# The last normalisation's mean and variance, on ScalarE in two passes and one step later

## The reference, cut to what matters

```python
x = _layernorm(x + decoder_layer(x))        # inside: h = ln(x + attn); ln(h + ffn(h))
x = _layernorm(x + expert_layer(x))         # the change concerns this norm
def _layernorm(x, axis=-1, eps=1e-05):
    m = jnp.mean(x, axis=axis, keepdims=True)
    v = jnp.var(x, axis=axis, keepdims=True)
    return (x - m) / jnp.sqrt(v + eps)
```

## Time and profile before

| | |
|---|---|
| median of 3 runs | 413.44 us (413.07 to 413.97) |
| the profiled execution's own time | 413.25 us |
| its span, first to last instruction | 411.5 us |
| PE / DVE / POOL / ACT busy | 91% / 80% / 61% / 52% |

### The profile page before, as it was taken

The page is one execution under the profiler, slowest core; times in us unless marked ns, Lnnn a source line. Parts: engine busy times, 40 slices in busy tenths (PEclk is TensorE's granted clock), DMA queues, the critical chain, the costliest instruction groups (busy, mean ns, idle before and its releaser), DMA issues. The chain is left out here.

```text
span 411.5 us, 6629 instructions
## 1 busy us (share of the span) xinstructions
PE 374.3 (91%) x2082; PEld 261.3 (64%) x2082; DVE 330.2 (80%) x789; ACT 215.9 (52%) x397; POOL 252.3 (61%) x431
## 2 busy tenths in 40 slices
PE   8897889788999999989998999899998998999992
PEld 3554556475847776677757884787567764955651
DVE  3649965699589987999799978998899979844543
ACT  2240316327844487527951896358652883276450
POOL 2017235896189836984599538983798459955231
PEclk9999999899999999999999999999999999999998
DMA  8236006500090006400370018100730045000000
GB/s 262 115 70 161 1 2 142 140 2 0 18 220 21 0 2 156 126 2 0 87 195 2 1 37 209 40 0 2 171 86 0 2 105 125 2 2 26 0 27 26
DMA packets 19875, 26.59 MB, mean 65 GB/s; under 512 B 1664, under 2 KB 9984, under 8 KB 19840
## 3 DMA queue, kind: packets, MB, share of 16 engines
q1 hardware_dynamic: 19696, 25.96, 24.7%
q10 hardware_dynamic: 144, 0.21, 0.2%
HBM read 7.29 MB, written 2.10 MB: 23 GB/s over the span
## 5 line engine op out<-in xcount | busy, mean ns | idle before, releaser
L892 POOL TENSOR_TENSOR prod<-cum_kv,q_fac 128x512 f32<-128x512 f32 x64 | 92.3, 1453 | 31.5 <-DVE cum_kv L1098 24.7
L412 PEld LDWEIGHTS pO<-s_wor,prod 128*128 128x128 f32 x512 | 62.9, 193 | 33.1 <-POOL prod L892 20.5
L412 PE MATMUL pO<-s_wor,prod 128*128 128x128 f32 x512 | 70.2, 283 | 13.3 <-POOL prod L892 13.2
L1092 DVE TENSOR_TENSOR kv<-k,vb 128x512 f32<-128x512 f32 x64 | 52.9, 827 | 6.7 <-DMA vb<-vs 6.7
L879 POOL TENSOR_TENSOR var_eps<-mv,s_con 128x4 f32<-128x4 f32 x32 | 9.5, 297 | 64.5 <-DVE mv L1120 64.5
L1098 DVE TENSOR_TENSOR_SCAN cum_kv<-p_ones,cum_kv,kv 128x512 f32<-128x512 f32 x32 | 40.5, 1275 | 0.6
L1098 DVE TENSOR_TENSOR_SCAN cum_kv<-p_ones,kv 128x512 f32<-128x512 f32 x32 | 38.6, 1214 | 0.5
L687 ACT ACTIVATE v<-pA,s_att 128x512 f32<-128x512 f32 x7 | 4.8, 687 | 62.4 <-PE pA L348 62.4
L517 PE MATMUL pY<-s_moe,gel 128*128 128x128 f32 x256 | 33.0, 276 | 0.0
L517 PEld LDWEIGHTS pY<-s_moe,gel 128*128 128x128 f32 x256 | 31.0, 192 | 2.9 <-issue 1.9
L882 POOL TENSOR_TENSOR rstd<-var_eps,s_con 128x4 f32<-128x4 f32 x32 | 32.5, 1016 | 0.0
(11 more groups left out here) (165 smaller groups left out, 813.1 us busy)
## 6 DMA issues: line engine op xcount, KB each, us to landing
vb<-vs SPq DMA_DIRECT2D x64, 256.0 KB, 4.7
xT<-x_t SPq DMA_DIRECT2D x8, 256.0 KB, 4.3
xt<-x SPq DMA_DIRECT2D x8, 256.0 KB, 5.0
out<-y SPq DMA_DIRECT2D x7, 256.0 KB, 2.3
s_moe<-moe_w SPq DMA_DIRECT2D x1, 836.0 KB, 10.1
s_wor<-wo_rep SPq DMA_DIRECT2D x1, 512.0 KB, 8.2
s_ffn<-ffn_w SPq DMA_DIRECT2D x1, 512.0 KB, 8.7
s_con<-consts SPq DMA_DIRECT2D x1, 502.0 KB, 4.8
```

Source lines behind the costliest of these rows:

```text
L412: mm = pe.matmul(pO3[:, s, :], prod[:, m % 4, s * P:(s + 1) * P], s_wor[:, m, :], start=False, stop=(m == DH - 1), skip_group_check=True)
L892: pool.tensor_tensor(prod[:, m % 4, :], cum_kv[t.par][:, m, :], q_fac[t.par][:, :], ALU.mult).then_inc(prod_ready, 1)
L1092: dve.tensor_tensor(kv[:, m % 3, :], k[t.par][:, :], vb[:, m, :], ALU.mult).then_inc(kv_ready, 1)
```

## The change

Tiles 0 to 4 get their norm 3 in another way and one step later (e = s-3). DVE still writes the residual, now into one of two buffers by the tile's parity, but takes no moments of it. In the next step ACT copies the four pieces into the output buffer y (which is overwritten later) with the sum over the features as accumulated output, POOL makes -mean and a bias from the sums, ACT squares the centred pieces with an accumulated output, which is the variance, POOL makes the inverse standard deviation and the shift, and ACT normalises. Tiles 5, 6 and 7 keep the old way.

```diff
+LATE_NORMS = TILES - 3
...
-        res = [None, None] + [sb(f"res{i}", [P, SUB, P]) for i in (2, 3)]
+        res = [None, None, sb("res2", [P, SUB, P]), None]
+        res3 = [sb(f"res3_{i}", [P, SUB, P]) for i in range(2)]
...
+        def late_norm(t):
+            return t.n < LATE_NORMS
+        def vector_norms(t, i):
+            return t.n - LATE_NORMS if i == 3 else t.n
... SP, step
-                if D: store(d)
+                if E and late_norm(e): store(e)
+                if D and not late_norm(d): store(d)
... ACT
+            def sum_residual(t):
+                act.wait_ge(res_ready[3], t.n + 1)
+                act.wait_ge(y_free[t.par], 16 * (t.slot_uses + 1))
+                for s in range(SUB):
+                    act.activation(y[t.par][:, s, :], res3[t.par][:, s, :], ACT.Copy,
+                                   accum_out=r_sum[:, s:s + 1]).then_inc(rsum_ready, 1)
+            def square_residual(t):
+                act.wait_ge(rsum_ready, SUB * (t.n + 1))
+                act.wait_ge(rbias_ready, t.n + 1)
+                for s in range(SUB):
+                    act.activation(y[t.par][:, s, :], res3[t.par][:, s, :], ACT.Square, bias=r_bias[:, s:s + 1],
+                                   scale=P ** -0.5, accum_out=r_var[:, s:s + 1]).then_inc(rvar_ready, 1)
... ACT, last_step
-                relu(d, 2); relu(d, 3)
-                normalise(c, 2); x2T_out(c); gate_exp(c)
+                relu(d, 2)
+                sum_residual(e)
+                relu(d, 3)
+                normalise(c, 2); x2T_out(c)
+                square_residual(e)
+                gate_exp(c)
...
                 u1T_out(c); gated_constant(c); udT_out(c)
+                normalise(e, 3)
... ACT, step
                 if A: q_out(a)
+                if E: sum_residual(e)
                 if D: relu(d, 3)
                 if A: k_out(a)
                 if C: normalise(c, 2); x2T_out(c)
+                if E: square_residual(e)
                 if A: v_out(a)
...
-                if D: normalise(d, 3)
+                if E: normalise(e, 3)
+                if D and not late_norm(d): normalise(d, 3)
... POOL
+            def residual_mean(t):
+                pool.wait_ge(rsum_ready, SUB * (t.n + 1))
+                wait(pool, norm_ready[3], SUB * t.n)
+                pool.tensor_tensor(neg_mean[3][:, :], r_sum[:, :], con("mean"), ALU.mult).then_inc(negmean_ready[3], 1)
+                pool.tensor_tensor(r_bias[:, :], r_sum[:, :], con("root"), ALU.mult).then_inc(rbias_ready, 1)
+            def residual_inverse_std(t):
+                pool.wait_ge(rvar_ready, SUB * (t.n + 1))
...                 (var+eps, pow and shift as in inverse_std)
... POOL, step
-                if B: product(b, 3); product(b, 4); product(b, 5); product(b, 6); product(b, 7); shifted_x(b)
+                if B: product(b, 3); product(b, 4)
+                if E and late_norm(e): residual_mean(e)
+                if B: product(b, 5); product(b, 6); product(b, 7); shifted_x(b)
                 if D: constant_residual(d)
                 if B: inverse_std(b, 0); scaled_h(b); h_residual(b)
+                if E and late_norm(e): residual_inverse_std(e)
                 if A: e_normal(a); attention_input(a)
-                if D: inverse_std(d, 3)
+                if D and not late_norm(d): inverse_std(d, 3)
                 if B: inverse_std(b, 1)
... DVE, expert_residual
-                wait(dve, norm_ready[3], SUB * t.n)
+                wait(dve, norm_ready[3], SUB * (t.n - 1))
... DVE, step
-                if D: piece_moments(d, 3)
+                if D and not late_norm(d): piece_moments(d, 3)
                 if A: values(a)
-                if D: join_moments(d, 3)
+                if D and not late_norm(d): join_moments(d, 3)
```

More of the change, by code:

```diff
@@ L31 @@
            "prefer": (896, 928), "mhalf": (928, 932), "lneps": (932, 936), "restart": (936, 1000),
-           "minus": (1000, 1004)}
+           "minus": (1000, 1004), "mean": (1004, 1008), "root": (1008, 1012)}
 ROWS = {"bo": 0, "g1": 1, "b1n": 2, "b2": 3, "g2": 4, "b2n": 5, "bffn": 6}
@@ L79, in build @@
         s_att = sb("s_att", [P, 415])
-        s_con = sb("s_con", [P, 1004])
+        s_con = sb("s_con", [P, 1012])
         s_wor = sb("s_wor", [P, DH, P])
@@ L154, in build @@
         x_b2n = sb("x_b2n", [P, SUB, P])
-        res = [None, None] + [sb(f"res{i}", [P, SUB, P]) for i in (2, 3)]
+        res = [None, None, sb("res2", [P, SUB, P]), None]
+        res3 = [sb(f"res3_{i}", [P, SUB, P]) for i in range(2)]
+        r_sum, r_bias, r_var = (sb(n, [P, SUB]) for n in ("r_sum", "r_bias", "r_var"))
         stats = [sb(f"stats{i}", [P, SUB, 6]) for i in range(4)]
@@ L192, in build, with residual @@
         res[0], res[1] = pO3, pY3
+        def residual(t, i):
+            return res3[t.par] if i == 3 else res[i]
+        def late_norm(t):
+            return t.n < LATE_NORMS
+        def vector_norms(t, i):
+            return t.n - LATE_NORMS if i == 3 else t.n
         def v_bank(t):
@@ L249, in build @@
         shift_ready = [sem(f"shift_ready{i}") for i in range(4)]
+        rsum_ready, rbias_ready, rvar_ready = sem("rsum_ready"), sem("rbias_ready"), sem("rvar_ready")
         norm_ready = [sem(f"norm_ready{i}") for i in range(4)]
@@ L316, in step @@
             def step(s):
-                a, b, c, d = s.plus(1), s, s.plus(-1), s.plus(-2)
-                A, B, C, D = a.exists(), b.exists(), c.exists(), d.exists()
+                a, b, c, d, e = s.plus(1), s, s.plus(-1), s.plus(-2), s.plus(-3)
+                A, B, C, D, E = a.exists(), b.exists(), c.exists(), d.exists(), e.exists()
                 if B: spread_vs(b, 4); spread_vs(b, 5); spread_vs(b, 6)
@@ L729, in normalise @@
                 for s in range(SUB // 2 if (i == 3 and t.n == TILES - 1) else SUB):
-                    act.activation(dst[:, s, :], res[i][:, s, :], ACT.Identity, bias=shift[i][:, s:s + 1],
+                    act.activation(dst[:, s, :], residual(t, i)[:, s, :], ACT.Identity, bias=shift[i][:, s:s + 1],
                                    scale=rstd[i][:, s:s + 1]).then_inc(norm_ready[i], 1)
+            def sum_residual(t):
[10 more added lines that the diff above has]
+                                   scale=P ** -0.5, accum_out=r_var[:, s:s + 1]).then_inc(rvar_ready, 1)
             def h_out(t):
@@ L830, in last_step @@
             def last_step(b):
-                c, d = b.plus(-1), b.plus(-2)
-                relu(d, 2); relu(d, 3)
-                normalise(c, 2); x2T_out(c); gate_exp(c)
+                c, d, e = b.plus(-1), b.plus(-2), b.plus(-3)
+                relu(d, 2)
[4 more added lines that the diff above has]
+                gate_exp(c)
                 normalise(b, 0); h_out(b); gelu(b, 0); gelu(b, 1)
@@ L875, in _ @@
         def _(pool):
+            def residual_mean(t):
[5 more added lines that the diff above has]
+                pool.wait_ge(rvar_ready, SUB * (t.n + 1))
+                pool.tensor_tensor(var_eps[3][:, :], r_var[:, :], con("lneps"), ALU.add).then_inc(vareps_ready[3], 1)
+                pool.wait_ge(vareps_ready[3], t.n + 1)
+                pool.tensor_tensor(rstd[3][:, :], var_eps[3][:, :], con("mhalf"), ALU.pow).then_inc(rstd_ready[3], 1)
+                pool.wait_ge(negmean_ready[3], t.n + 1)
+                pool.wait_ge(rstd_ready[3], t.n + 1)
+                pool.tensor_tensor(shift[3][:, :], neg_mean[3][:, :], rstd[3][:, :], ALU.mult).then_inc(shift_ready[3], 1)
             def inverse_std(t, i):
-                pool.wait_ge(mv_ready[i], SUB * (t.n + 1))
+                pool.wait_ge(mv_ready[i], SUB * (vector_norms(t, i) + 1))
                 wait(pool, norm_ready[i], SUB * t.n)
@@ L1109, in piece_moments @@
                         dve.wait_ge(res_ready[2], SUB * t.n + s + 1)
-                    dve.bn_stats(stats[i][:, s, :], res[i][:, s, :]).then_inc(stats_ready[i], 1)
+                    dve.bn_stats(stats[i][:, s, :], residual(t, i)[:, s, :]).then_inc(stats_ready[i], 1)
             def moments(t, i):
@@ L1116, in join_moments @@
             def join_moments(t, i):
-                dve.wait_ge(stats_ready[i], SUB * (t.n + 1))
+                dve.wait_ge(stats_ready[i], SUB * (vector_norms(t, i) + 1))
                 dve.memset(fence[:, :], 0.0)
@@ L1203, in expert_residual @@
                 dve.wait_ge(x2c_ready, t.n + 1)
-                wait(dve, norm_ready[3], SUB * t.n)
+                wait(dve, norm_ready[3], SUB * (t.n - 1))
                 for s in range(SUB):
-                    ins = dve.scalar_tensor_tensor(res[3][:, s, :], pY3[:, s, :], gate_sum[t.par][:, s:s + 1],
+                    ins = dve.scalar_tensor_tensor(res3[t.par][:, s, :], pY3[:, s, :], gate_sum[t.par][:, s:s + 1],
                                                    x2c[:, s, :], ALU.mult, ALU.add)
@@ L1236, in closing @@
                 for s in range(SUB // 2, SUB):
```

(4 more changed lines are left out.)

## The result

The changed kernel takes 418.07 us (median of 4, 417.22 to 418.58) against 413.3 us (413.07 to 413.97): ratio 1.0111, interval 1.009 to 1.0132. The forecast was 416.3 us, with a range of 414.9 to 417.9. A second series gave 417.29 us (median of 5, 416.81 to 418.25) beside 413.37 us: 1.0096, 1.008 to 1.0112. The profiled execution took 417.96 us, 4.7 us more than that of the kernel before, with a span of 416.2 us.

What follows compares the result with a forecast made beforehand. The prediction took DVE's scans and PE to limit each step in turn. 413.25 us + 0 for the steps + 2.87 for the last step gave 416.1, by the median 416.3 us; range 414.9 to 417.9.

Steps and rivals of the forecast that it cites:

- What bounds: In a middle step: DVE's scans limit at about 256 to 268 us, PE from 268 to 295 us.
- What comes off DVE: Norm 3's moments: 1.43 us per late tile, 7.2 us over five; counted as 0 because both following waits end with PE.
- rival B: DVE's relief counts because scans begin earlier; in full -7.2 us, 409.1 us; chance 0.04 in full or enough to win.
- Sums: Four accumulating copies on ACT before relu(d, 3), steps 3 to 6: 0.5 us each, 2.0 us together, cost 0.
- the cover: PE's 1.12 us of waiting for POOL's products hides ACT's four sums up to 2.5 us per step.
- Squares: Four accumulating squares on ACT after x2T_out: 2.0 us, hidden while v_out waits for PE; cost 0.
- Buffers and constants: Second residual buffer removes a wait never open; eight more constant columns add under 0.1 us to one load: 0.
- The new wait: Last step: POOL's inverse_std(5, 3) waits for ACT's tile 4, delaying tile 7's norm 1; 2.87 us, bounds 2.0 and 3.4.
- The pauses: PE's new waits ahead of x2_T in the last step: 1.2, 0.8 and 1.3 us, with work between.
- D: Rival, chance 0.05: PE's new pauses in the last step lower the clock; about 1.7 us more, 418.0 us.
- A: Rival, chance 0.08: ACT's four sums cost more than 2.5 us; at 0.8 us a piece, 419.1 us in all.
- C: Rival, chance 0.05: tile 7 does not feel the last step's wait since PE holds it back anyway; 413.4 us.

Runs made afterwards that it cites:

- e4: The changed kernel with norm 3's bn_stats and bn_aggr back on DVE for tiles 0 to 4, into buffers nobody reads: 416.95 us.
- e6: The changed kernel with ACT's four summing activations issued three times, the additional sets into spare buffers: 417.70 us.
- e8: The changed kernel with no late tile, keeping the two residual buffers, weaker wait and extra constant columns: 413.42 us, ratio 0.9996.
- e1: The changed kernel with ACT's normalise(4, 3) in the last step moved ahead of u1T_out(6): 413.38 us, ratio 0.9989; repeated, 413.42 us.
- e2: The changed kernel with POOL's inverse_std(b, 1) placed ahead of inverse_std(d, 3): 415.34 us, ratio 1.0038.
- e7: The changed kernel with four late tiles instead of five: 416.66 us, ratio 1.0078.
- e5: The changed kernel with ACT's four summing activations issued twice, the additional set into spare buffers: 417.68 us.

## Why the forecast was right in kind and 1.8 us short

- What bounds: PE behind DVE's two waits. Right (e4). What comes off DVE was put too high, 1.43 us a tile for a measured 1.1: I had added up busy times of instructions that overlap. Step 1 of the kernel before, which has no norm 3, already had waits of 1.82 and 1.10 us. Since the term counted as 0, it cost nothing; the bound of -7.2 us in rival B would have been -5.4.
- Sums: 0.29 us a piece, not 0.5. The read of the accumulator, which I bounded by the 202 ns of table_probe, is there with 190 ns but overlaps its neighbours. Cost in the step 0, as forecast; the size of the cover was too small (e6).
- Squares, residual_mean, residual_inverse_std, store: 0, as forecast (the steps are no longer). Buffers and constants: 0 (e8). Product 5 started at once behind r_bias, whose operation took 0.72 us, and product 7 was on time.
- The new wait: forecast 2.87 us, measured 2.83. POOL at 374.98 (forecast 374.7, and 0.2 us of it is start-up), x2_T at 386.44 (386.2). e1 shows by taking it away that it is the cause (of the fall of the clock too, since PE's pauses go with it), e2 that POOL's order is the larger part, e7 that it goes with the hand-over.
- The pauses: 1.17, 0.69 and 1.06 us (forecast 1.2, 0.8, 1.3). Here is the step that failed: the sum had nothing for the clock. I priced the fall as a rival of its own, D, at 5% and 418.0 us, with the Trainium skill's clock rule ("TensorE: Matmul & The Clock Gate", Part 1) beside it, and had only a pause of 2.77 us to go by the earlier trace rows. D's price was right, 1.7 us for a measured 1.6, and its chance was far too low: over nine executions each, filling two of the pauses saves 1.4 us in the mean. So the term belonged into the sum at nearly its full size. The trace agrees with that rule in the half clock, 1.2 GHz in the slowed stretch; but the rule as I cited it speaks of an idle stretch, and what stood ahead of the fall here were short pauses with work between, so "by that rule alone 418.0" claimed more than it gives.
- The median of 418.07 us is 0.17 us above the range, and by the traces it has the fall of the clock in it. Without it the forecast holds: 416.81 us in the profiled execution that had no fall in its closing, 416.33 and 416.44 us in the two series with the filler.
- Rivals A, B and C are out: A, since four sums took 1.17 us and even two sets were free (e5); B by e4; C by the 2.83 us.

## What to carry to other kernels

When a stage is moved later for some items and not for others, look at the first item of the old kind behind the last of the new: single buffers make it wait for the moved work, and what waits in that queue behind it pays. Work taken off a busy engine is worth only what its next wait gives back; look at what ends that wait. And count a new pause of PE twice, once for its length and once, with a chance, for the clock behind it.

## What the runs showed of the hardware

A fall of the granted clock from 2.4 to 1.2 GHz followed PE's pauses of 1.17, 0.69, 1.06 and 0.69 us; it cost 1.6 us and appeared in two of five profiled executions with these pauses. With two of the pauses filled, none of nine executions was above 416.9 us. The same comes and goes elsewhere. Near 98 us PE has pauses of 1.18 and 0.74 us with and without the change: in the profiled executions of e1 and e2 a fall followed (eight matmuls took 1.86 and 1.92 us), in that of the kernel before none did (1.06 us). And of e6's four pauses of about 2 us one had a fall behind it, for 1.2 us. So the length of one pause did not decide it.

ScalarE's accumulated output is an instruction of its own, 190 ns, that overlaps the activations around it, but not at no cost as far as the rows go: squares with one per-partition operand and an accumulated output start 0.39 us apart, c_gate's copies with one such operand and none 0.29 us. That is 0.10 us a piece, if Square and Copy cost the same otherwise, which no run separates. The summing copies, without a per-partition operand, start 0.29 us apart, 1.17 us for four.
